# Norm boundary and feed-forward written out as one pipeline over chunks, in two places, with two smaller moves of work

## What is computed

```
x = hidden_states                                  # (2, 1024, 256)
y = attention_0(layernorm(x))                      # 16 heads of 128, rope, causal softmax, Wo
x = x + layernorm(y)
y = bitlinear(sigmoid(bitlinear(n, w1)) * bitlinear(n, w2), w3)   # n = layernorm(x), width 704
x = x + layernorm(y)                               # bitlinear: weights quantised to -1, 0, 1
y = attention_1(layernorm(x))                      # 32 query heads on 8 key heads, width 8
x = x + layernorm(y)
y = (silu(n @ w_gate.T) * (n @ w_up.T)) @ w_down.T                # n = layernorm(x), width 1024
x = x + layernorm(y)
```

## Time and profile before

| what | value |
|---|---|
| median of 3 runs | 1905.16 us (1902.91 to 1907.54) |
| the profiled execution's own time | 1904.82 us |
| its span in the trace | 1903.1 us |
| PE busy / PEld / DVE / ACT / POOL | 1654.3 / 1020.7 / 1383.8 / 1129.0 / 667.5 us |
| PE's share of the span | 87% |
| traffic through the hardware queue | 60.55 MB, 13.1% of 16 engines |

### The profile page before, as it was taken

The page is one execution under the profiler, slowest core; times in us unless marked ns, Lnnn a source line. Parts: engine busy times, 40 slices in busy tenths (PEclk is TensorE's granted clock), DMA queues, the critical chain, the costliest instruction groups (busy, mean ns, idle before and its releaser), DMA issues. The chain is left out here.

```text
span 1903.1 us, 43770 instructions
## 1 busy us (share of the span) xinstructions
PE 1654.3 (87%) x14612; PEld 1020.7 (54%) x14612; DVE 1383.8 (73%) x2882; ACT 1129.0 (59%) x2158; POOL 667.5 (35%) x756
## 2 busy tenths in 40 slices
PE   3899999999999999999827745899999999982997
PEld 1577777777777777777713422233333333341554
DVE  4487777778777777777766564888888888837564
ACT  4566666666666666666545641266666666666444
POOL 0654554555455555545221123021212222223011
PEclk9899999999999999999968967899999999995998
DMA  4322111112111111211000010000000000001000
GB/s 130 88 54 49 41 47 43 43 41 52 47 41 47 44 41 41 52 47 34 17 0 1 1 36 9 17 13 15 15 13 16 12 18 11 8 1 66 1 23 22
DMA packets 53107, 61.83 MB, mean 32 GB/s; under 512 B 11345, under 2 KB 32018, under 8 KB 53010
## 3 DMA queue, kind: packets, MB, share of 16 engines
q1 hardware_dynamic: 53010, 60.55, 13.1%
HBM read 18.57 MB, written 2.10 MB: 11 GB/s over the span
## 5 line engine op out<-in xcount | busy, mean ns | idle before, releaser
L1566 ACT ACTIVATE a_prob<-psum 128x1024 f32<-128x1024 f32 (+3 forms) x384 | 302.3, 813 | 212.1 <-PE psum L1523 209.5
L1606 DVE TENSOR_REDUCE a_mx<-psum 128x1 f32<-128x512 f32 (+3 forms) x608 | 367.5, 655 | 61.2 <-PE psum L1505 55.0
L1598 POOL TENSOR_SCALAR_AFFINE_SELECT a_prob<-a_prob 128x256 f32<-128x256 f32 x256 | 103.8, 406 | 420.5 <-ACT a_prob L1566 418.0
L1502 PE MATMUL psum<-a_kd,a_qp 128*128 128x512 f16 (+3 forms) x768 | 217.5, 337 | 34.2 <-DMA a_kd<-a_k_part 22.6
L528 POOL TENSOR_TENSOR a_swp<-a_swp,a_sin 128x512 f32<-128x512 f32 x128 | 163.1, 1274 | 161.6 <-DMA a_swp<-a_lin 161.6
L884 DVE TENSOR_REDUCE a_nmax<-psum 128x1 f32<-128x1024 f32 (+7 forms) x256 | 191.3, 748 | 1.0 <-PE psum L599 1.0
L532 POOL TENSOR_TENSOR a_rope<-a_swp,a_cosd 128x512 f32<-128x512 f32 x128 | 164.2, 1283 | 12.4 <-POOL a_swp L528 4.7
L224 POOL TENSOR_TENSOR x<-x,y (+1 forms) x64 | 54.4, 879 | 319.5 <-ACT y L196 319.5
L1544 PE MATMUL psum<-a_prob,a_vg 128*32 128x512 f32 (+3 forms) x1536 | 165.4, 503 | 0.8 <-ACT a_o_sb L1572 0.4
L1502 PEld LDWEIGHTS psum<-a_kd,a_qp 128*128 128x128 f16 x768 | 70.7, 98 | 173.3 <-DVE a_mx L1606 94.4
L756 ACT ACTIVATE a_prob_big<-psum,a_nmax 128x1024 f32<-128x1024 f32 (+3 forms) x128 | 121.8, 952 | 68.5 <-DVE a_nmax L884 65.1
(11 more groups left out here) (256 smaller groups left out, 4477.8 us busy)
## 6 DMA issues: line engine op xcount, KB each, us to landing
a_swp<-a_lin SPq DMA_DIRECT2D x256, 128.0 KB, 2.3
a_qp<-a_q_part SPq DMA_DIRECT2D x192, 16.0 KB
a_kd<-a_k_part SPq DMA_DIRECT2D x192, 16.0 KB
x<-_attn_hidden_states_dram SPq DMA_DIRECT2D x4, 512.0 KB, 5.5
a_w_raw<-in_L_attn_Wq_dram SPq DMA_DIRECT2D x16, 128.0 KB, 2.3
a_w_raw<-in_L_attn_Wk_dram SPq DMA_DIRECT2D x16, 128.0 KB, 2.3
a_w_raw<-in_L_attn_Wv_dram SPq DMA_DIRECT2D x16, 128.0 KB, 2.3
a_wo_raw<-in_L_attn_Wo_dram SPq DMA_DIRECT2D x1, 2048.0 KB
```

The costliest lines, as they stand in the source:

```text
L1502: last = pe.matmul(to[:, j * n:(j + 1) * n], qp[:, w % 3, t * P:(t + 1) * P], kd[:, w % 3, j0 + j, a:e], start=True, stop=not edge)
L1566: act.activation(prob_at(u, i)[:, 2 * pair:2 * pair + 2, a % BANK:a % BANK + e - a], c.psum[:, pair_of(u, i):pair_of(u, i) + 2, 0:e - a], ...
L1606: dve.tensor_reduce(mx[:, t, j0:j0 + per, a // BANK], work(("S", w, i))[:, 0:per * (e - a)].rearrange("p (j n) -> p j n", j=per), AX.X, AL ...
```

## The change

`boundary("mid1")` with `ffn("f0")`, and `boundary("mid3")` with `ffn("f1")`, are each replaced by one function, `normed_ffn`, in one block and with no loops: every instruction of the four chunks is written out. Its order on each engine is fixed by hand. `gate_up(ch, ht)` is the gate and up product of a hidden tile, `turn(ch)` the transposes of a chunk, `down(ch)` the down product. The norm of `y` is taken over two groups of eight tiles instead of four of four, and GpSimd scales twelve of the sixteen tiles itself with a `tensor_scalar`. `x` is normalised chunk by chunk while the chunk before is in the feed-forward. `down(ch - 1)` stands after the second hidden tile of chunk `ch`. The hidden parts and `xn` have two buffers. The down product writes two tiles into a PSUM bank, and the result is read with two instructions of 512 columns instead of four of 256. The weights are prepared in three pieces (`pieces`: the first half of gate and up, the second half, then down).

The weights of f1 are loaded in boundary "mid2", behind the first loads of attention 1 on the same queue, instead of at the start of "mid3", and their buffer is held through attention 1. In attention 0 both `vals` calls move behind `context` of their step.

```diff
-            weights = Quantise(c, raw, wctx)
-            boundary(c, "mid1", True, weights, unit=WSCALE)
-            ffn(c, "f0", raw.tiles, weights.parts, 1.0, True)
-        c.end_phase()
-        attention_1(c, ins, lambda loads: boundary(c, "mid2", False, Loads(loads)))
+            normed_ffn(c, "f0", Ternary(c, raw, wctx), WSCALE, 1.0, True)
...
-            weights = LoadAndSplit(c, raw, wctx)
-            boundary(c, "mid3", True, weights)
-            ffn(c, "f1", raw.tiles, weights.parts, 1.0 / WSCALE, False, out)
+
+            def with_weights(loads):
+                boundary(c, "mid2", False, Loads(lambda sp: (loads(sp), raw.load(sp))))
+            attention_1(c, ins, with_weights)
+            c.end_phase()
+            normed_ffn(c, "f1", HighLow(c, raw, wctx), 1.0, 1.0 / WSCALE, False, out)
...
                         if p == 1 and exists(u - 1):
                             pe.wait_ge(y_done, 4 * (u - 1) + 2)
                             out(u - 1, h - 1 + b, 2)
-                        if p == 2 and exists(u + 1):
-                            if exists(u - 1):
-                                pe.wait_ge(y_done, 4 * (u - 1) + 3)
-                            else:
-                                pe.wait_ge(cos_ready, 5)
-                            vals(u + 1, h + b, 1 - b, 0)
-                        if p == 3 and exists(u + 1):
-                            if exists(u - 1):
-                                pe.wait_ge(y_done, 4 * (u - 1) + 4)
-                            else:
-                                pe.wait_ge(cos_ready, 8)
-                            vals(u + 1, h + b, 1 - b, 1)
                         if p == 4 and exists(u + 2):
...
+                        if p == 2 and exists(u + 1):
+                            if exists(u - 1):
+                                pe.wait_ge(y_done, 4 * (u - 1) + 3)
+                            else:
+                                pe.wait_ge(cos_ready, 5)
+                            vals(u + 1, h + b, 1 - b, 0)
+                        if p == 3 and exists(u + 1):
+                            if exists(u - 1):
+                                pe.wait_ge(y_done, 4 * (u - 1) + 4)
+                            else:
+                                pe.wait_ge(cos_ready, 8)
+                            vals(u + 1, h + b, 1 - b, 1)
...
+class Moments:
...
+    def statistics(self, dve, src, t0, t1):
+        for t in range(t0, t1):
+            dve.bn_stats(self.stats[:, t, :], src[:, t:t + 1, :]).then_inc(self.stats_ready, 1)
...
+    def root(self, act, g):
+        t0, t1 = self.groups[g]
+        act.wait_ge(self.var_ready, g + 1)
+        act.activation(self.sd[:, t0:t1], self.var[:, t0:t1], ACT.Sqrt).then_inc(self.sd_ready, 1)
...
+        for n, (j, cols) in enumerate(self.raw.pieces(piece)):
+            dve.tensor_scalar(self.raw.view(self.below, j)[:, :, cols], self.raw.view(self.raw.buf, j)[:, :, cols],
+                              self.neg[:, j:j + 1], None, ALU.is_lt).then_inc(self.below_ready, 1)
+            dve.wait_ge(self.below_ready, 2 * piece + n + 1)
+            dve.scalar_tensor_tensor(out=self.raw.view(self.ternary, j)[:, :, cols], in0=self.raw.view(self.raw.buf, j)[:, :, cols],
+                                     scalar=self.pos[:, j:j + 1], in1=self.raw.view(self.below, j)[:, :, cols],
+                                     op0=ALU.is_gt, op1=ALU.subtract).then_inc(self.ready, 1)
...
+    def scalar(self, act, piece):
+        if piece == 0:
+            act.wait_ge(self.raw.loaded, self.raw.landed)
+        for j, cols in self.raw.pieces(piece):
+            act.activation(self.parts[j][0][:, :, cols], self.raw.view(self.raw.buf, j)[:, :, cols], ACT.Copy,
+                           scale=WSCALE).then_inc(self.hi_made, 1)
...
+def normed_ffn(c, name, weights, y_unit, unscale, sigmoid_only, out=None):
...
+        y_norm = Moments(c, f"{name}_y", [(0, NT // 2), (NT // 2, NT)], ctx, y_unit)
+        x_norm = Moments(c, f"{name}_x", by_chunk, ctx)
+        e_norm = Moments(c, f"{name}_e", by_chunk, ctx)
...
+                def gate_up(ch, ht):
+                    s = ch * HT + ht
+                    if ht == 0:
+                        pe.wait_ge(lo_ready, 2 * ch + 2)
+                    if ch == 0 and ht in (0, HT // 2):
+                        pe.wait_ge(weights.ready, 2 if ht == 0 else 4)
+                    wait(pe, hid_ready, s - 1)
...
+                weights.tensor(pe)
+                turn(0)
+                for ch in range(CHUNKS):
+                    for ht in range(HT):
+                        gate_up(ch, ht)
+                        if ht == 1 and ch >= 1:
+                            down(ch - 1)
+                        if ht == 2 and ch + 1 < CHUNKS:
+                            turn(ch + 1)
+                down(CHUNKS - 1)
...
+                def sigmoid(s):
+                    act.wait_ge(gate_made, s + 1)
+                    wait(act, hid_ready, s - 1)
+                    act.activation(sig[:, s % 2, :], hidden(0, s), ACT.Sigmoid, scale=unscale).then_inc(sig_ready, 1)
...
+                weights.scalar(act, 0)
+                y_norm.root(act, 0)
+                scale_y()
+                weights.scalar(act, 1)
+                weights.scalar(act, 2)
+                x_norm.root(act, 0)
+                scale_x(0)
+                y_norm.root(act, 1)
+                high(0)
+                for ch in range(CHUNKS):
+                    for ht in range(HT):
+                        s = ch * HT + ht
+                        sigmoid(s)
+                        if s >= 1:
+                            hidden_high(s - 1)
+                        if ht == 0 and ch + 1 < CHUNKS:
+                            x_norm.root(act, ch + 1)
+                        if ht == 0 and ch >= 2:
+                            e_norm.root(act, ch - 2)
+                        if ht == 1 and ch + 1 < CHUNKS:
+                            scale_x(ch + 1)
+                        if ht == 1 and ch >= 1:
+                            result(ch - 1)
+                        if ht == 2 and ch + 1 < CHUNKS:
+                            high(ch + 1)
+                hidden_high(NS - 1)
+                e_norm.root(act, CHUNKS - 2)
+                result(CHUNKS - 1)
+                e_norm.root(act, CHUNKS - 1)
...
+                def product(s):
+                    dve.wait_ge(sig_ready, s + 1)
...
+                    wait(dve, hid_lo, s - 1)
+                    dve.tensor_tensor(hid[:, s % 2, :], hidden(1, s), g, ALU.mult).then_inc(hid_ready, 1)
...
+                y_norm.statistics(dve, c.y, 0, NT // 2)
+                y_norm.variance(dve, 0)
+                y_norm.normaliser(dve, 0)
+                y_norm.statistics(dve, c.y, NT // 2, NT)
+                x_variance(0)
+                x_norm.normaliser(dve, 0)
+                y_norm.variance(dve, 1)
+                weights.vector(dve, 0)
+                low(0)
+                y_norm.normaliser(dve, 1)
+                weights.vector(dve, 1)
+                for ch in range(CHUNKS):
+                    for ht in range(HT):
+                        s = ch * HT + ht
+                        product(s)
+                        if s >= 1:
+                            hidden_low(s - 1)
+                        if ht == 0 and ch + 1 < CHUNKS:
+                            x_variance(ch + 1)
+                        if ht == 1 and ch + 1 < CHUNKS:
+                            x_norm.normaliser(dve, ch + 1)
+                        if ht == 1 and ch >= 2:
+                            e_norm.normaliser(dve, ch - 2)
+                        if ht == 2 and ch + 1 < CHUNKS:
+                            low(ch + 1)
+                        if ht == 3 and ch == 0:
+                            weights.vector(dve, 2)
+                        if ht == 3 and ch >= 1:
+                            e_variance(ch - 1)
+                hidden_low(NS - 1)
+                e_norm.normaliser(dve, CHUNKS - 2)
+                e_variance(CHUNKS - 1)
+                e_norm.normaliser(dve, CHUNKS - 1)
...
+                for t in range(TPC):
+                    pool.wait_ge(y_normed, t + 1)
+                    add_y(t)
+                for t in range(TPC, NT):
+                    if t == NT // 2:
+                        pool.wait_ge(y_norm.norm_ready, 4)
+                    pool.tensor_scalar(c.y[:, t:t + 1, :], c.y[:, t:t + 1, :], y_norm.rstd[:, t:t + 1], y_norm.shift[:, t:t + 1],
+                                       ALU.mult, ALU.add).then_inc(y_scaled, 1)
+                    pool.wait_ge(y_scaled, t - TPC + 1)
+                    add_y(t)```

The matrix engine in a unit of attention 0, at p = 2 (`a_w_*` are the projection weights, `a_pt_*` the probabilities, `a_v_*` the values; L599 is the last matmul of `score`). Before:

```order
L599 MATMUL psum<-mask_qk,ident_b 128x128
...
L576 MATMUL psum<-a_w_hi,xT_hi 128x128
L576 MATMUL psum<-a_w_lo,xT_hi 128x128
```

(9 more changed lines are left out.)

303 lines of the change are left out of this document (163 added, 140 removed).

## The result

The changed kernel takes 1845.8 us (median of 4 runs, 1844.86 to 1846.37) against 1904.05 for the kernel before in the same measurement: a ratio of 0.969, with a 95% interval of 0.967 to 0.971. The prediction was 1838 us, with a range of 1824 to 1862. The profiled execution took 1844.86 us with a span of 1843.1, so 60.0 us of span are gone where 67.1 were forecast.

The account below looks back on a forecast made before the run. The matrix engine was taken as nearly always busy, so gains lie only in its waits, in attention 0 and both seams: 1904.8 - 24 - 23.7 - 19.8 + 0.4 = 1837.7, predicted 1838 us, range 1824 to 1862.

Parts of the forecast that it names:

- Attention 0: Value projections behind `context`, which covers the matrix engine's repeated wait for y: 30 gaps of about 0.79 us, -24 us.
- The rival in which another wait takes its place: Attention 0 keeps its period because another wait, most likely `vals` again, replaces the removed one: 1862 us, chance 0.15.
- Seam one, first gate: Mid1 into f0: first gate matmul 17.8 us after the seam's first statistics, against 49.0 before, -31.2 us.
- Costed at nothing: GpSimd's `tensor_scalar` (0.4 to 1.25 us a tile), early load of f1's weights and tail steps taken as covered, except 0.2 per tail.
- Seam one, chunk 0: First chunk of f0, with a return at 1.2 GHz and the third weight piece ahead of product 4: 22.4 us.
- Chunks 1 and 2: In f0, each set by a chain over DVE and ACT: 19.9 us, against 16.5 of matrix engine work.
- looser: 17 handovers between ACT and DVE per chunk cost 0.2 us more each: 1851 us, chance 0.17.
- tighter: Sigmoids and low parts overlap better, f0's second and third chunks run at 16.5 to 17.5 us: 1828 us, chance 0.12.
- End of f0: Last chunk without transposes, then the last down 5.2 us with 2.4 of waits for low parts: 23.3 us.
- Seam two: Mid3 into f1: first gate matmul at 16.9 against 45.8, then matrix engine bound for 136.7 against 127.5: -19.8 us.
- the rival with a drain: Each ACT table switch costs 1.4 us beyond its 1.28 load, adding 6 to 8: 1845 us, chance 0.05.
- Weights and tail: Early f1 weight load covered by boundary and projections, nothing; tail after the last matmul keeps its steps, 0.2 us per seam.

Follow-up runs that it names:

- `v_alone`: The kernel before with only both `vals` calls moved behind `context` of their step: 1880.0 us, ratio 0.9874 to the kernel before.

## Why the prediction was nearly right, and what it missed

**Attention 0**: right in cause and nearly in size. 24 forecast, 23.3 in the profile after and 22.7 in that of `v_alone`, whose runs are 24.3 faster as a whole. A unit gains 0.76 as forecast, and the last interval gives 1.0 back. The rival in which another wait takes its place is out: none of the waits left occurs more than four times.

**Seam one, first gate**: forecast 17.8, measured 19.5. y's scaling starts at 5.1 and GpSimd's first four adds end at 8.5, both as worked out. Then x's variance takes 1.8 instead of 0.8, and y's second one 1.4, also instead of 0.8. The step that failed is the one headed "Costed at nothing": GpSimd's `tensor_scalar` was bounded by when its tiles would be late (0.55 measured, bounds 0.4 and 1.25, and it was never late), and not by what it does to the vector instructions beside it. With GpSimd held, the two first gates were 17.8 and 16.9, the forecast to 0.1 us.

The trace of before had the price. The forecast took 2.2 us for statistics and variance from the first four tiles of mid1, during which GpSimd was idle. The next four took 3.3. Here are instructions of their variance, beside GpSimd's adds, and the same instruction a little later with GpSimd idle:

```profile
973.56 0.69 DVE L171 TENSOR_TENSOR mid_y_mdif<-mid_y_stats 128x4 f32<-128x4 f32 x1
974.28 0.65 DVE L172 TENSOR_SCALAR mid_y_m<-mid_y_m 128x4 f32<-128x4 f32 x1
...
976.75 0.16 DVE L171 TENSOR_TENSOR mid_x_mdif<-mid_x_stats 128x4 f32<-128x4 f32 x1
```

The first two end at 974.25 and 974.93. The four adds of the earlier trace rows run from 972.13 to 974.90.

**Seam one, chunk 0**: forecast 22.4, measured 24.8. By the rows 2.0 of the 2.4 is the same cause, in the second weight piece and in chunk 1's variance and normaliser, and without GpSimd there it is 22.7. The forecast also added up wrongly by 0.2: 17.8 + 1.1 + 3.2 is 22.1 and not 21.9. The wait for scaled x was 6.3 us and not about 4.

**Chunks 1 and 2**: forecast 19.9, measured 20.05 and 20.2. The chain was right, the rival "looser" (0.2 at each of 17 handovers) is out by its size, and so is "tighter": that rival became true only when the order was changed, at 17.5 to 18.

**End of f0**: forecast 23.3, measured 25.3, of which 1.7 is the lower clock in the last down. An execution without it would have come out at 23.6. The forecast had the 2.4 us of waits, and gave the clock a price at the start of a chunk but none here.

**Seam two**: first gate 18.1 against 16.9, GpSimd again. The wait for scaled x in chunk 0 was 6.0 instead of 4.6, and 4.1 with GpSimd held there, so that is its work too. That the matrix engine bounds the rest was right: chunks 1 and 2 of f1 take 32.07 us in every version, and from the first gate to the end it is 137.9 against 136.7.

**Table switches**: the rival with a drain is out, and the forecast by the rows stands. **Weights and tail**: nothing that could be measured was lost, as costed.

Together, GpSimd beside DVE is 1.7 + 2.0 + 1.2 us, and the clock in the last down 1.7: 6.6 of the 8.9 that the two seams fell short. In f1's chunk 0 holding GpSimd gave 2.1 more, while only 1.2 were missing behind the first gate: from there to the end it is then 135.8 against the forecast's 136.7, so something in that sum was costed 0.9 too high, and what, is open. That the profiled execution fell only 7.1 us short in all, and not 8.9, is the luck of its start-up.

## What to carry to other kernels

When work moves to GpSimd, price two things: its own time, and each vector instruction with which it will overlap. The trace of before had both: the small instructions shown above, and four adds that took 2.77 us, but 5.00 beside the vector engine's weight pieces. A place for such work is where the vector engine waits, and not beside the small instructions that head a chain. But the tiles must still come in time: held until the first low parts GpSimd gained nothing, held for tiles 8 to 15 alone it gained 3 us. In a pipeline written out by hand, look for an engine that is idle inside the critical chain, the instructions that wait for each other and so set the time (DVE for 2.2 us while ACT loads a table here) and move the next link of the chain into it: one line moved gave 10 us, more than all that the forecast had missed.

## What the runs showed that was not expected

The smallest vector instructions pay most: 0.16 us became up to 0.73, while statistics of four tiles kept their 1.40 us beside the same GpSimd work. The same program lost 1.7 us to the clock in its last down in some executions only. And of 60 us, 2.2 were in the start-up ahead of the first `a_ctx_hi`, which differs by up to 3.6 us between executions of equal code; the stretch from f0's end to seam two differs by 3.1 (granted clock 0.96 or 0.97 in attention 1). Parts smaller than that must be read from their own stage, as here, and not from the whole time.
